# One-hot maps, running counts and ranks of the expert routing, worked out per group of four tiles inside the routing stage

## What is computed

```
logits = x2 @ router_w
scores = jax.nn.softmax(logits, axis=-1)
expert_weights, expert_indices = lax.top_k(scores, top_k)
flat_e = expert_indices.reshape(-1)
flat_t = jnp.repeat(jnp.arange(T), top_k)
order = jnp.argsort(flat_e)
xs = x2[flat_t[order]]
...
ys = lax.ragged_dot(jax.nn.silu(gate) * up, wd, group_sizes)
return jnp.zeros_like(x2).at[tok].add(ys * flat_w[order][:, None])
```

## Time and profile before

| | us |
|---|---|
| executions timed | 4291.42, 4291.71, 4296.32 |
| their median | 4291.71 |
| span of the profiled execution | 4296.5 |
| `phase_route` in it | 1771.7 to 1880.0 |
| `phase_slots` in it | 1880.3 to 1936.4 |
| last scatter of group 0 ends | 2002.3 |
| first matmul of the experts | 2007.7 |

### The profile page before, as it was taken

One profiled execution on the slowest core, in us unless ns is written; L12 is line 12 of the kernel. 1 busy time (PEld: TensorE's weight loads), 2 busy tenths in 40 slices (PEclk: granted clock), 3 DMA queues, 4 the chain that ended last, 5 costly groups with the idle time before them and its releaser, 6 DMA issues. The chain is left out here.

```text
span 4296.5 us, 115371 instructions
## 1 busy us (share of the span) xinstructions
PE 3510.7 (82%) x41173; PEld 1852.0 (43%) x41175; DVE 2485.8 (58%) x5229; ACT 2102.7 (49%) x4024; POOL 1149.9 (27%) x2368
## 2 busy tenths in 40 slices
PE   8699999999999999732396977550869699898999
PEld 5232222322323222332264644440757566544678
DVE  7788888888888888580021238457245433235433
ACT  2488888888888888421143434320610022264322
POOL 1222222222222221124505844510533123210000
PEclk9799999999999999866698988555965599898999
DMA  1000000000000002534346533344723300233353
GB/s 53 7 6 6 6 6 7 6 6 6 6 7 6 6 6 89 189 102 139 136 137 195 161 118 124 122 140 150 246 84 75 86 15 0 84 135 125 108 188 125
DMA packets 288679, 345.07 MB, mean 80 GB/s; under 512 B 36768, under 2 KB 201632, under 8 KB 288544
## 3 DMA queue, kind: packets, MB, share of 16 engines
q1 hardware_dynamic: 254736, 297.27, 21.7%
q0 software_dynamic: 13328, 37.77, 2.7%
q10 hardware_dynamic: 20480, 8.40, 0.7%
HBM read 198.11 MB, written 135.79 MB: 78 GB/s over the span
## 5 line engine op out<-in xcount | busy, mean ns | idle before, releaser
L945 DVE TENSOR_REDUCE att_maxes<-att_ps_m 128x1 f32<-128x512 f32 x2048 | 1308.5, 686 | 230.9 <-PE att_ps_m L789 225.2
L900 ACT ACTIVATE att_prob<-att_ps_s 128x512 f32<-128x512 f32 x2048 | 1105.6, 599 | 222.5 <-PE att_ps_s L799 209.9
L799 PE MATMUL att_ps_s<-att_q_t,att_k_t 99*128 99x512 bf16 x2048 | 687.2, 386 | 8.7 <-ACT att_prob L900 7.9
L810 PE MATMUL att_ps_o<-att_prob,att_v_h 128*32 128x512 f32 x4096 | 546.4, 605 | 0.7 <-ACT att_prob L900 0.7
L787 PE MATMUL att_ps_m<-att_k_t,att_q_t 48*128 48x512 bf16 x1024 | 398.8, 389 | 16.3 <-DVE att_maxes L945 11.5
L789 PE MATMUL att_ps_m<-z_sb 48*128 48x512 bf16 x1024 | 399.3, 390 | 0.0
L787 PEld LDWEIGHTS att_ps_m<-att_k_t,att_q_t 48*128 48x128 bf16 x1024 | 94.6, 92 | 610.3 <-DVE att_maxes L945 509.8
L1570 DVE TENSOR_TENSOR experts_h<-experts_gs,experts_ps_g 128x128 f32<-128x128 f32 x192 | 55.3, 288 | 497.4 <-ACT experts_gs L1551 423.5
L698 POOL CAST att_max_parts<-att_neg_max 128x4 bf16<-128x4 f32 x128 | 24.9, 194 | 1154.1 <-DVE att_neg_max L952 1154.1
L799 PEld LDWEIGHTS att_ps_s<-att_q_t,att_k_t 99*128 99x128 bf16 x2048 | 157.7, 96 | 281.0 <-ACT att_prob L900 134.4
L1523 PE MATMUL experts_ps_g<-w_gu,experts_x_t 128*128 x768 | 225.1, 417 | 54.8 <-issue 41.0
(11 more groups left out here) (357 smaller groups left out, 6472.0 us busy)
## 6 DMA issues: line engine op xcount, KB each, us to landing
xf_t<-logits_t SPq DMA_DIRECT2D x16, 2048.0 KB, 8.5
slots_x<-zeros SPq DMA_DIRECT2D x97, 256.0 KB, 3.3
experts_xs<-slots_x SPq DMA_DIRECT2D x48, 512.0 KB
slots_y<-experts_y SPq DMA_DIRECT2D x48, 512.0 KB
logits_t<-sstat_logit SPq DMA_DIRECT2D x64, 256.0 KB
proj<-comb_pr SPq DMA_DIRECT2D x8, 1600.0 KB
mix_pr<-proj SPq DMA_DIRECT2D x32, 400.0 KB
gram_qk_in<-proj SPq DMA_DIRECT2D x32, 256.0 KB
```

The source lines that it names most:

```text
L799: pe.matmul(ps_s[bank(p, i)][:, :], k_t[0:ROWS, p, tile * P:(tile + 1) * P], q_t[0:ROWS, p, chunk * W:(chunk + 1) * W], start=True, stop=T ...
L810: mm = pe.matmul(ps_o[i * VW:(i + 1) * VW, :], v_h[:, p, group * GK + i, :], prob[:, (j * GK + i) % (RING * GK), :], start=(group == 0), s ...
L900: nc.scalar.activation(prob[:, i % (RING * GK), :], ps_s[bank(p, i)][:, :], ACT.Exp, scale=SCALE).then_inc(expd.sem, 1)
L945: v.tensor_reduce(maxes[:, p, tile, c:c + 1], ps_m[bank(p, i)][:, :], X, ALU.max).then_inc(reduced.sem, 1)
```

## The change

Five things are done.

1. The one-hot maps (`hot`, now bf16), their sum `both` and the running count `before` are made in `phase_route`, for each group at the end of `top`.
2. A third step is added to the pipeline of `phase_route`: PE's `count(t)` gives the ranks of a group's tokens in the second half of the same PSUM buffer that holds its logits, and DVE's `place(t)` multiplies them by `hot` and sums over the experts, which gives `rank`.
3. PE's `route(t)` also waits for `place(t - 2)`, which reads the buffer that it is about to write.
4. `phase_slots` starts with the totals. It multiplies `hot` by the first rows, sums (`start`), and adds `rank`, for group 0 first and then for group 1. `work` and `gap` come behind both.
5. POOL starts the scatters once group 0's `pos` is there, and `SCATTERS_EARLY` goes from 14 to 30.

```diff
             def top(t, p):
...
+                v.wait_ge(topped.sem, topped.at(t))
+                hold(v, gate)
+                for r in range(TOPK):
+                    v.tensor_tensor(hot[r][:, bass.ds(t * GT, GT), :, :].rearrange("q t g e -> q (t g) e"),
+                                    idx_f[:, :, :, r:r + 1].rearrange("q t g k -> q (t g) k").to_broadcast([P, GT * G, E]),
+                                    iota_e[:, :].unsqueeze(1).to_broadcast([P, GT * G, E]), ALU.is_equal).then_inc(chosen.sem, 1)
+                v.wait_ge(chosen.sem, chosen.at(t, TOPK))
+                hold(v, gate)
+                v.tensor_tensor(both[:, p, :, :], hot[0][:, bass.ds(t * GT, GT), :, :].rearrange("q t g e -> q t (g e)"),
+                                hot[1][:, bass.ds(t * GT, GT), :, :].rearrange("q t g e -> q t (g e)"), ALU.add).then_inc(chosen.sem, 1)
+                for i in range(GT):
+                    v.wait_ge(chosen.sem, chosen.at(t, TOPK + 1 + i))
+                    hold(v, gate)
+                    v.tensor_tensor(flat(before[:, bass.ds(t * GT + i + 1, 1), :]), flat(before[:, bass.ds(t * GT + i, 1), :]),
+                                    both[:, p, i, :], ALU.add).then_inc(chosen.sem, 1)
+
+            def place(t, p):
+                v.wait_ge(counted.sem, counted.at(t))
+                hold(v, gate)
+                v.wait_ge(ranked.sem, ranked.before(t, 1))
+                hold(v, gate)
+                for r in range(TOPK):
+                    v.tensor_tensor(own[:, r, :, :, :].rearrange("q t g e -> q t (g e)"), ps_l[p][:, :, GE:2 * GE],
+                                    hot[r][:, bass.ds(t * GT, GT), :, :].rearrange("q t g e -> q t (g e)"), ALU.mult).then_inc(ranked.sem, 1)
+                v.wait_ge(ranked.sem, ranked.at(t, TOPK))
+                hold(v, gate)
+                for r in range(TOPK):
+                    v.tensor_reduce(rank[:, bass.ds(t * GT, GT), :, r:r + 1].rearrange("q t g a -> q (t g) a"),
+                                    own[:, r, :, :, :].rearrange("q t g e -> q (t g) e"), X, ALU.add).then_inc(ranked.sem, 1)
+            staged(v, N, normalise, top, place)
...
             def route(t, p):
...
                 pe.wait_ge(topped.sem, topped.before(t))
+                hold(pe, gate)
+                pe.wait_ge(ranked.sem, ranked.before(t))
...
+            def count(t, p):
+                pe.wait_ge(chosen.sem, chosen.at(t))
+                pe.matmul(ps_l[p][:, :, GE:2 * GE], tri[:, :], both[:, p, :, :], start=True, stop=False)
+                pe.matmul(ps_l[p][:, :, GE:2 * GE], ones[:, :], before[:, bass.ds(t * GT, GT), :],
+                          start=False, stop=True).then_inc(counted.sem, 1)
+            staged(pe, N, project, route, count)
...
 def phase_slots
...
-            for t in range(NT):
-                settle()
-                did(v.tensor_tensor(before[:, t + 1, :], before[:, t, :], both[:, t, :], ALU.add))
...
-            did(v.tensor_copy(pos[:, :, :, :], pos_f[:, :, :, :]), "pos")
+            for g in range(G):
+                for r in range(TOPK):
+                    did(v.tensor_tensor(at_start[r][:, :, g, :], hot[r][:, :, g, :],
+                                        starts[:, g, :].unsqueeze(1).to_broadcast([P, NT, E]), ALU.mult))
+                settle()
+                for r in range(TOPK):
+                    did(v.tensor_reduce(start[:, :, g, r:r + 1], at_start[r][:, :, g, :], X, ALU.add))
+                settle()
+                did(v.tensor_tensor(pos[:, :, g, :], rank[:, :, g, :], start[:, :, g, :], ALU.add), f"pos{g}")
...
-            pool.wait_ge(step, n["pos"])
+            pool.wait_ge(step, n["pos0"])
...
-SCATTERS_EARLY = 14
+SCATTERS_EARLY = 30
```

More of the change, by code:

```diff
@@ L987, with phase_route @@
 SLOTS = SLOT_TILES * P
-def phase_route(nc, sems, x, o_sb, out_w, out_b, routers, x1_sb, xn_sb, lg_sb, top_val, top_idx, ident,
+def phase_route(nc, sems, x, o_sb, out_w, out_b, routers, x1_sb, xn_sb, lg_sb, top_val, hot, before, rank, ones, ident,
                 w_gu, first_experts, w_landed):
@@ L1056, in _ @@
             pool.memset(neg_half[:, :], -0.5).then_inc(half_set, 1)
+            pool.iota(iota_e[:, :], pattern=[[1, E]], base=0, channel_multiplier=0,
+                      allow_small_or_imprecise_dtypes=True).then_inc(made, 1)
+            pool.memset(ones[:, :], 1.0).then_inc(made, 1)
+            pool.memset(tri[:, :], 1.0).then_inc(made, 1)
+            pool.wait_ge(made, 3)
+            pool.affine_select(out=tri[:, :], in_=tri[:, :], compare_op=ALU.is_gt, fill=0.0, base=0,
+                               pattern=[[1, P]], channel_multiplier=-1).then_inc(made, 1)
             pool.wait_ge(half_set, 1)
@@ L1140, in _ @@
         def _(v):
-            for s in (x1_ready, norm, topped):
+            for s in (x1_ready, norm, topped, chosen, ranked):
                 s.prime(v)
+            v.memset(before[:, 0, :], 0.0).then_inc(before_set, 1)
+            v.wait_ge(before_set, 1)
+            v.wait_ge(made, 4)
             def normalise(t, p):
@@ L1181, in phase_slots @@
+            staged(v, N, normalise, top, place)
+def phase_slots(nc, sems, lg_sb, top_val, hot, before, rank, ones, weight, pos, tile_expert, xn_sb, slots_x, scattered):
     TE = SLOT_TILES + 1
     with Phase(nc, "slots", sems) as ph:
-        iota_e = ph.sb("iota_e", [P, E])
         iota_t = ph.sb("iota_t", [1, TE])
[L1185 to L1188, removed]
@@ L1189, in phase_slots @@
-        tri = ph.sb("tri", [P, P], BF16)
-        ones = ph.sb("ones", [P, P], BF16)
         work = ph.sb("work", [P, NT, G, E])
-        place = ph.sb("place", [P, NT, G, E])
+        at_start = [ph.sb(f"at_start{r}", [P, NT, G, E]) for r in range(TOPK)]
         gap = ph.sb("gap", [P, NT, G, TOPK])
@@ L1268, in _ @@
             settle()
[L1269 to L1273, removed]
-                                    starts[:, :, :].rearrange("q g e -> q (g e)").unsqueeze(1).to_broadcast([P, NB, GE]),
-                                    ALU.add))
-            settle()
@@ L1288, in _ @@
+            v.wait_ge(made, 1)
             for g in range(G):
@@ L3453, in two_layers @@
                 top_val = held(routed, "top_val", [P, NT, G, TOPK])
[L3454 removed]
+                hot = [held(routed, f"hot{r}", [P, NT, G, E], BF16) for r in range(TOPK)]
+                before = held(routed, "before", [P, NT + 1, GE], BF16)
+                rank = held(routed, "rank", [P, NT, G, TOPK])
+                ones = held(routed, "ones", [P, P], BF16)
                 phase_route(nc, layer, x, z_sb, t["L0_attn_out_w"], t["L0_attn_out_b"],
[L3456 removed]
+                            [t[f"L0_ffn_router_w{g}"] for g in range(G)], x_sb, z_sb, lg_sb, top_val, hot, before, rank, ones, ident,
                             w_gu, experts[0], w_landed)
[L3458 removed]
+                phase_slots(nc, layer, lg_sb, top_val, hot, before, rank, ones, weight, pos, tile_expert, z_sb, slots_x, scattered)
             w_d = [held(ctx, "w_d", [P, E, D]), z_sb]
```

76 lines of the change are left out of this document (22 added, 54 removed).

## The result

The changed kernel took 4311.5 us (median of 4 runs, 4307.1 to 4313.7) against 4292.6 for the kernel before (4 runs, one more than the three above, 4291.4 to 4296.3). The ratio is 1.0041, 95% interval 1.0026 to 1.0055: 18.9 us slower where 16.3 were forecast, and inside the range. The profiled execution of the changed kernel took 4307.1 us, the shortest of the four.

A forecast was written before the change was run, and what follows sets the result against it. DVE was taken to pace `phase_route`, POOL's scatters what follows; 38.4 us added there plus 2.9 of stalls less 25.0 in `phase_slots` gave +16.3, from 4291.7 to 4308.0 us, range 4296 to 4316.

The forecast's parts named there:

- first `route_x` to the barrier: `phase_route` grows by 38.4 us: six passes at 5.21 us each, 31.3, plus 7.1 at its end.
- `phase_slots` to the first scatter: From the first memset to the first scatter, 7.6 us remain of 32.6: 25.0 us less.
- first to last scatter: POOL's row of scatters gets 2.9 us longer, as more of them wait for DVE's two-input products.
- the steps: DVE work added per `phase_route` pass: 1.87 us for `hot`, `both` and `before`, 1.50 for `place`.
- the gaps: Idle time ahead of eight DVE steps per `phase_route` pass that wait behind a `hold`: 0.23 us each.
- the stalls: Scatters starting inside DVE's two-input SBUF products wait for their end: 7.9 to 10.2 us instead of 6.0.
- the short-gap rival: In `phase_route`, gaps of only 0.03 us each: total +4.2 us, 4295.9, no measurable change; chance 17%.
- the end of the stage: End of `phase_route`: later last logits, the last `top` part and two `place` add 7.1 us.
- The hidden case: PE sets the pace of `phase_route`, added DVE steps fill holes: total -15.0 us, 4276.7; chance 6%.
- the PE case: PE at its lower clock becomes the bound in longer `phase_route` passes: total +21.6 us, 4313.3; chance 15%.

The follow-up runs named there:

- e1: Changed kernel with four more dependent DVE steps shaped like `before` in every group, whose result nothing reads: 4320.2 us, ratio 1.0063 to the kernel before.
- e5: Changed kernel with `both` and the four `before` of a group moved from DVE to POOL: 4290.8 us, ratio 0.9998 to the kernel before.
- e7: Changed kernel without the six `hold(v, gate)` lines of the new DVE steps: 4305.9 us, ratio 1.0032 to the kernel before.
- e3: Changed kernel with the two `past` products reading their ends from PSUM instead of SBUF: 4307.2 us, ratio 1.0033 to the kernel before.
- f4: Changed kernel with 14 early scatters as before instead of 30: 4310.5 us, ratio 1.0044 to the kernel before.
- f3: Kernel before with POOL's bias addition held back, `phase_slots` ordered by expert group with bf16 maps, and `past` reading from PSUM: 4266.9 us, ratio 0.9942.
- e2: Changed kernel with POOL's bias addition held until the normalisation two groups before is done: 4299.3 us, ratio 1.0015 to the kernel before.
- e6: Kernel before with only POOL's bias addition held until the normalisation two groups before is done: 4278.0 us, ratio 0.9967.
- e4: Kernel before with only `phase_slots` ordered by expert group, bf16 maps and 30 early scatters; maps, counts and ranks stay there: 4287.4 us, ratio 0.9990.

## Why the prediction was right

Term by term, from the two profiles of the changed kernel (first, second), each with its own starts:

| term | forecast | measured |
|---|---|---|
| start of the first `route_x` | 0 | +0.7, +1.5 |
| first `route_x` to the barrier | +38.4 | +34.7, +36.7 |
| `phase_slots` to the first scatter | -25.0 | -25.2, -25.2 |
| first to last scatter | +2.9 | +3.2, +3.0 |
| last scatter to the first matmul | 0 | 0.0, 0.0 |
| sum | +16.3 | +13.4, +16.1 (by the starts) |

The sign, the steps, the gaps and the stalls were rightly foreseen, but that the second profile's +16.1 comes so near to +16.3 is in part luck. `phase_route` grew there by 1.7 us less than forecast, and the first term, put at nothing, made up for 1.5 of it. That term is there in every profile: the first `route_x` starts at 1786.9 to 1787.2 in the kernels without the moved part and at 1787.5 to 1789.3 in those with it. PE's first matmul of the stage is late already, at 1776.84 and 1777.39 for 1776.16. Why, no run shows.

**What bounds the kernel.** DVE in `phase_route`, POOL behind the first scatter: e1, e5 and e7 moved DVE's share in both directions and the passes followed, and from the fourth group on `route_x` did not wait for PE in any profile.

**The steps.** A pair at 0.76 for 0.75, `both` at 0.29 for 0.35, `before` at 0.19. **The gaps** were the choice that told this forecast from no measurable change: 1.9 to 2.1 us for the eight of a pass, with 1.8 forecast and 0.24 for the short-gap rival. That rival is out, and e7 shows what part of them is the `hold`. The rule in the Trainium skill's page "VectorE: DVE Perf Modes" (Rules for kernel authors) that it is operations that count and not semaphores does not hold for these: between the dependent `before` steps in the loop the gaps of 0.25 us and more are longer than the steps of 0.19.

**The first profile's shortfall.** `phase_route` grew by 34.7 there, 3.7 less than forecast. 2.0 of it are one pass in which POOL's addition missed `route_xn`. The fourth and the fifth group's in DVE's timeline of the first profile, then the fifth in the second:

```profile
1831.19 3.43 DVE L214 TENSOR_SCALAR route_xn<-route_x,route_mv,route_rstd 128x256 f32<-128x256 f32 x4 [1.13 <-POOL route_rstd L1083]
...
1847.71 1.38 DVE L214 TENSOR_SCALAR route_xn<-route_x,route_mv,route_rstd 128x256 f32<-128x256 f32 x4 [1.13 <-POOL route_rstd L1083]
```

```profile
1848.61 3.41 DVE L214 TENSOR_SCALAR route_xn<-route_x,route_mv,route_rstd 128x256 f32<-128x256 f32 x4 [1.13 <-POOL route_rstd L1083]
```

The two POOL rows beside them say why:

```profile
1832.12 2.35 POOL L1079 TENSOR_TENSOR route_x_in<-route_x_in,route_bias 128x1024 f32<-128x1024 f32 x1 [0.97 <-DMA route_x_in<-in_L_attn_x]
...
1848.73 2.57 POOL L1079 TENSOR_TENSOR route_x_in<-route_x_in,route_bias 128x1024 f32<-128x1024 f32 x1 [1.05 <-DMA route_x_in<-in_L_attn_x]
```

POOL started 0.93 us behind `route_xn` in the one and 1.02 us in the other, where it was POOL's addition that took longer, 2.57 for 2.35. In the other profiles `route_xn` is still held up at 0.97 us: a landing less than 0.1 us later decides over 2 us. The rest, 1.7 us, is missing in the second profile too. Of that, 1.1 are the idle times of 0.55 and 0.53 us ahead of two `route_x` at the turn of the loop, which have fallen away, and 0.4 are the end of the stage. That registers are now worked out beside the steps that stand there is argued, not shown.

**The end of the stage.** Forecast 7.1; from the last `rank` in the loop (1902.1) to the end of the stage (1915.4) it is 13.3 us, for 6.6 before: 6.7 more.

**The scatters.** Four stalls of 1.0, 1.9, 2.4 and 3.0 us, 8.3, lie within the 7.9 to 10.2 of the prediction; e3 shows the mechanism. They are 2.3 us more than before, so the measured +3.2 and +3.0 hold some 0.7 of another kind: the pause at the barrier, 4.59 us for 3.92, which the prediction put at nothing (f4). The Trainium skill's page "SBUF — State Buffer" (Who interferes with whom) says that a tensor_tensor with two operands in SBUF holds up GpSimd's reads, and these stalls agree. Its inference that the generation of descriptors is not held up would leave such DMAs alone, and here they are held up; but these indirect DMAs also read `pos`. Which of POOL's accesses waits, no run here tells apart.

**The hidden case** asked for PE as the pace, and **the PE case** for projections late at the lower clock. The granted clock did fall, 0.97 to 0.73, and to 0.63 in the pass from 1873.87 to 1888.02, with a projection of 5.70 us for 3.71:

```profile
1880.32 5.70 PE L1109 MATMUL route_ps_y<-route_w_t,route_turn_t 128*128 128x256 f32 x16 [0.68 <-ACT route_turn_t L1153]
1888.02 1.22 DVE L1177 TENSOR_TENSOR route_x<-route_ps_y,route_x_in 128x1024 f32<-128x1024 f32 x1
```

The lead of PE shrank there from the 5.4 us of before to 2.0, but it was not used up. This case had the right clock, and was 2 us from the consequence.

**What stays open.** The timed difference (18.9 and 20.3 us) lies 3 and 4 us above the 16.1 that the second profile's start of the experts shows, and within its interval (11 to 24, 15 to 27). How long the part behind that start takes differs by some us from profile to profile, with the longest in the kernel before and the shortest, 2278.8, in f3, whose time is otherwise explained; no run looked into it.

## What to carry to other kernels

Work moved from a serial stage into a pipelined one is hidden only if the engine it lands on is not the one that sets the pace there; DVE's 17% of idle time in two passes before looked like room and was none. Eight small groups of steps cost more than one wide pass over the same elements: a dependent step on 64 elements was 0.19 us of work behind a gap of 0.25. Before moving anything, look for steps whose duration has two values (here `route_xn`, 1.4 and 3.4 us): one such collision, in six of eight groups, was worth 13 us in the kernel before, half of what the moved part was to bring.

## What the runs showed of the hardware

A DVE tensor_scalar with both ends in SBUF waited for a POOL tensor_tensor that had started: four `route_xn` take 1.38 us alone (e2, e6) and 3.4 beside POOL's 2.35, and even `route_veps`, four elements wide, lasted 1.25 us instead of 0.17 until POOL was done (e5). DVE's work on PSUM went on beside POOL's addition: the eight MAX8 of the logits took 0.87 us there in e2, as in the earlier trace rows. An indirect DMA on POOL, 0.96 us as a rule, waits for a DVE product over two SBUF operands that runs when it starts (up to 3.98 us) and not for the same product with one operand in PSUM (e3). An addition of 64 bf16 elements takes 0.192 us on DVE and 0.30 on POOL; `both` over 2048 elements took 2.29 us from f32 maps and 1.23 from bf16 ones (e4).
